# An attention block on one core: the row shift goes to GpSimd, half of the normalising to ScalarE, small jobs one step later, and image 0's opening is reordered

## What is computed

```
# block 1, per image; N = 1024 pixels
pairwise = (theta_x @ phi_x) / N;   y = pairwise @ g_x
z = x + out_w @ y + out_b
# block 2, per image; c = 128
theta = t_w @ z + t_b;  phi = p_w @ z + p_b
scores = einsum('cp,cq->pq', theta, phi) / sqrt(c)
attn = softmax(scores, axis=-1)            # 1024 x 1024
out = z + conv1_w @ einsum('pq,cq->cp', attn, z) + conv1_b
```

## Time and profile before

| | us |
|---|---|
| median of three runs | 188.06 |
| the profiled execution, its own time | 187.35 |
| its span, first to last instruction | 185.6 |
| TensorE busy | 167.1 (90%) |
| VectorE busy | 140.6 (76%) |
| ScalarE busy | 100.4 (54%) |
| GpSimd busy | 34.9 (19%) |
| chain that ended last: PE, DVE, ACT | 46%, 31%, 14% |

### The profile page before, as it was taken

How to read it: one execution, slowest core, us unless ns; L and a number is a source line. 1 busy time by engine, 2 the same in 40 slices (tenths; PEclk the granted TensorE clock), 3 DMA queues, 4 the chain that set the end, 5 groups by cost and what they waited for, 6 DMA issues and landing times.

```text
span 185.6 us, 2628 instructions
## 1 busy us (share of the span) xinstructions
PE 167.1 (90%) x969; PEld 135.7 (73%) x969; DVE 140.6 (76%) x253; ACT 100.4 (54%) x183; POOL 34.9 (19%) x34
## 2 busy tenths in 40 slices
PE   7877647979999998999999998999999989997994
PEld 7656436867787877788778776877878768766794
DVE  1514847897898889677998899577998898888712
ACT  3235544367755672478665652467765736466420
POOL 1007000005300054018100081038000070020020
PEclk9999979999999999999999999999999999999999
DMA  5630000300000010000100010000100010001011
GB/s 138 174 113 4 0 0 0 113 2 4 0 2 0 0 58 2 0 0 4 57 0 0 0 60 0 0 2 0 60 2 0 0 57 4 0 0 57 0 60 57
DMA packets 2828, 4.75 MB, mean 26 GB/s; under 512 B 448, under 2 KB 1280, under 8 KB 2816
## 3 DMA queue, kind: packets, MB, share of 16 engines
q1 hardware_dynamic: 2304, 4.39, 6.8%
q10 hardware_dynamic: 512, 0.20, 0.6%
HBM read 2.49 MB, written 2.10 MB: 25 GB/s over the span
## 4 chain that ended last, share of the span: by engine, by line
PE 46%; DVE 31%; ACT 14%; issue 4%; DMA 3%; DVEq 0%; SPq 0%; ACTq 0%
PE numer L336 11%; DVE negmax L661 11%; DVE PT_lo L684 7%; ACT P L510 7%; PE turned L316 6%; DVE P L677 4%; PE ring L220 4%; PE aux L280 3%; PE ring L222 3%; PE ring L221 3%; ACT PT_hi L518 3%; DVE t_lo L641 3%; DMA X<-x_dram 3%; DVE shift L669 3%; PE aux L343 2%
## 5 line engine op out<-in xcount | busy, mean ns | idle before, releaser
L518 ACT ACTIVATE PT_hi<-turned 128x512 fp32r<-128x512 f32 x62 | 36.9, 595 | 35.5 <-PE turned L316 35.2
L684 DVE TENSOR_TENSOR PT_lo<-turned,PT_hi 128x512 fp32r<-128x512 f32 x62 | 42.5, 685 | 8.6 <-ACT PT_hi L518 8.4
L510 ACT ACTIVATE P<-ring,shift 128x1024 f32<-128x1024 f32 x32 | 35.7, 1117 | 20.8 <-DVE shift L669 19.4
L661 DVE TENSOR_REDUCE negmax<-ring 128x1 f32<-128x1024 f32 x32 | 38.9, 1217 | 5.9 <-PE ring L222 5.7
L316 PE MATMUL turned<-identity,P 128*128 128x128 f32 x256 | 38.8, 275 | 2.4 <-DVE P L677 2.2
L316 PEld LDWEIGHTS turned<-identity,P 128*128 128x128 f32 x256 | 31.0, 141 | 12.4 <-DVE P L677 5.5
L677 DVE TENSOR_SCALAR P<-P,rden 128x1024 f32<-128x1024 f32 x32 | 28.6, 894 | 1.1
L220 PE MATMUL ring<-Z_hi,t_hi 128*128 128x512 f32 x64 | 27.8, 434 | 0.7 <-DVE t_lo L721 0.7
L221 PE MATMUL ring<-Z_hi,t_lo 128*128 128x512 f32 x64 | 25.5, 398 | 0.0
L222 PE MATMUL ring<-Z_lo,t_hi 128*128 128x512 f32 x64 | 25.4, 398 | 0.0
L336 PE MATMUL numer<-PT_hi,V_hi 128*128 128x512 f32 x56 | 24.4, 435 | 0.5 <-issue 0.3
(11 more groups left out here) (117 smaller groups left out, 203.7 us busy)
## 6 DMA issues: line engine op xcount, KB each, us to landing
out_dram<-result SPq DMA_DIRECT2D x7, 256.0 KB, 2.1
X<-x_dram SPq DMA_DIRECT2D x3, 512.0 KB, 3.4
X<-x_dram SPq DMA_DIRECT2D x2, 256.0 KB, 3.9
out_dram<-result SPq DMA_DIRECT2D x1, 192.0 KB, 1.9
w<-weights_dram SPq DMA_DIRECT2D x1, 128.0 KB, 5.3
wi<-inner_dram ACTq DMA_DIRECT2D x1, 64.2 KB, 5.6
pg_w<-pg_weights_dram ACTq DMA_DIRECT2D x1, 64.0 KB, 3.2
pg_b<-pg_bias_dram ACTq DMA_DIRECT2D x1, 64.0 KB, 5.1
```

The costliest lines, as they stand in the source:

```text
L510: nc.scalar.activation(P[:, n % P_BUFFERS, :], ring[:, n % 2, :], ACT.Exp, bias=shift[:, t:t + 1], accum_out=den[:, t:t + 1]).then_inc(pro ...
L518: nc.scalar.activation(PT_hi[:, group % GROUPS, half_chunks(half), k * TILE:(k + 1) * TILE], turned[:, columns(half)].rearrange("p (j r) - ...
L661: nc.vector.tensor_reduce(negmax[:, t:t + 1], ring[:, n % 2, :], AX.X, ALU.max, negate=True).then_inc(max_ready, 1)
L684: nc.vector.tensor_tensor(PT_lo[:, group % GROUPS, half_chunks(half), rows], turned[:, columns(half)].rearrange("p (j r) -> p j r", j=CHUN ...
```

## The change

- **Row shift.** VectorE's `row_max` is only the maximum now. The shift goes to GpSimd (`row_shift`), put first into GpSimd's step n for tile n+2, in front of the longer work, which is spread over the steps: t = 0: `finish`, high part of X; 1 and 2: low part of X by halves; 4 and 5: `split_z`; 6: `finish`; in the last image `V_last` in step 2.
- **Normalising.** VectorE multiplies columns 0 to 511 only; ScalarE the others (`norm_half`), between the exponential of tile n+2 and the high part of the second turned half. Each half has its own semaphore for TensorE's `turn`.
- **Small jobs a step later.** t = 0: for image 0 alone the value parts 1 and 2; 1: pg0, pg1; 2: MT, R; 3: A, Z0; 4: Z1; 5: t0, V0; 6: V1, V2; 7: t1.
- **Opening.** X of image 0 is not split. Z comes from the float32 block-1 matrix `AT` and X, one float32 matmul for each half. R goes ahead of the weight transposes and A ahead of the products of the weights. TP and U are copied by VectorE instead of ScalarE, U is split by GpSimd instead of VectorE, and the float32 Z is put together by GpSimd from its parts, where ScalarE copied it from PSUM. Scores of tile 0 go ahead of the first value part; value parts 1 and 2 move from ahead of the loop into its step 0. VectorE takes `norm(0)` ahead of `row_max(1)`.

The diff, cut to its core (VectorE's and ScalarE's lists of jobs change as TensorE's does):

```diff
 
 
 JOBS = ("pg0", "pg1", "MT", "R", "A", "Z0", "Z1", "t0", "V0", "V1", "V2", "t1")
-FIRST_JOBS = ("MT", "R", "A", "t1")
+FIRST_JOBS = ("MT", "R", "A", "t1", "V2")
 
 
 def aux_before(b, job):
...
@@ -260,8 +263,7 @@
 
             def job_Z(b, half):
                 pe.wait_ge(aux_free, aux_before(b, f"Z{half}"))
-                if half == 0:
-                    pe.wait_ge(x_lo, b)
+                pe.wait_ge(x_lo, (b - 1) * HALVES + half + 1)
                 affine_half(aux[:, :], half).then_inc(aux_ready, 1)
 
             def queries(b, bank, cols):
...
@@ -308,8 +310,7 @@
                 mm.then_inc(scores_ready, 1)
 
             def turn(n, half):
-                if half == 0:
-                    pe.wait_ge(probs_normed, n + 1)
+                pe.wait_ge(probs_normed[half], n + 1)
                 if n >= 1:
                     pe.wait_ge(turned_lo, (n - 1) * HALVES + half + 1)
                 for j in half_range(half):
...
@@ -357,14 +357,15 @@
             mm.then_inc(aux_ready, 1)
 
 
+            pe.wait_ge(pad_ready, 2)
+            pe.wait_ge(wi_padded, 1)
+            pe.wait_ge(wi_loaded, 16)
+            job_R(0)
             pe.wait_ge(identity_ready, 2)
             pe.wait_ge(w_loaded, 16)
             nc.tensor.transpose(turned[:, 0:C], w[:, W_T:W_T + C], identity[:, :])
             nc.tensor.transpose(turned[:, C:2 * C], w[:, W_P:W_P + C], identity[:, :]).then_inc(tp_ready, 1)
-            pe.wait_ge(pad_ready, 2)
-            pe.wait_ge(wi_padded, 1)
-            pe.wait_ge(wi_loaded, 16)
-            job_R(0)
+            job_A(0)
             pe.wait_ge(tp_copied, 1)
             pe.wait_ge(bias_loaded, 16)
             theta_b, phi_b = bias[:, B_T:B_T + 1], bias[:, B_P:B_P + 1]
@@ -374,55 +375,59 @@
             nc.tensor.matmul(UT_bank[:, C + 1:C + 2], T_w, phi_b, start=True, stop=True)
             nc.tensor.matmul(UT_bank[:, C + 2:C + 3], theta_b.broadcast_to([C, C]), phi_b,
                              start=True, stop=True).then_inc(u_ready, 1)
-            job_A(0)
-            pe.wait_ge(aux_free, aux_after(0, "A"))
+            pe.wait_ge(first_a, 1)
             for half in range(HALVES):
-                pe.wait_ge(first_x_lo, half + 1)
-                affine_half(ring[:, 1, columns(half)], half).then_inc(first_z, 1)
+                nc.tensor.matmul(ring[:, 1, columns(half)], AT[:, :], X[:, 0, columns(half)],
+                                 start=True, stop=True).then_inc(first_z, 1)
 
             pe.wait_ge(u_lo, 1)
             pe.wait_ge(first_z_lo, 1)
             queries(0, first_t_bank(0), FIRST_T[0]).then_inc(first_t, 1)
+            scores(0)
             pe.wait_ge(first_z_ready, 1)
             pe.wait_ge(vw_ready, 2)
             pe.wait_ge(conv_loaded, 16)
             value_chunks(0, numer, 0).then_inc(first_v, 1)
-            scores(0)
             queries(0, first_t_bank(1), FIRST_T[1]).then_inc(first_t, 1)
             job_t(0, 1)
-            pe.wait_ge(first_z_ready, 2)
             scores(1)
-            for part in (1, 2):
-                pe.wait_ge(first_v_lo, part)
-                value_chunks(0, numer, part).then_inc(first_v, 1)
+
+            def first_value_part():
+                pe.wait_ge(first_z_ready, 2)
+                pe.wait_ge(first_v_lo, 1)
+                value_chunks(0, numer, 1).then_inc(first_v, 1)
 
             def job_one(b, t):
-                if t == 0:
+                if t == 0 and b == 1:
+                    first_value_part()
...
@@ -528,72 +533,70 @@
                 nc.scalar.activation(attended[:, group % GROUPS, :], numer[:, :], ACT.Identity,
                                      bias=bias[:, B_C:B_C + 1]).then_inc(numer_copied, 1)
 
-            for half in range(HALVES):
-                act.wait_ge(first_loaded[half], 16)
-                nc.scalar.activation(X_hi[:, columns(half)], X[:, 0, columns(half)], ACT.Copy).then_inc(first_x_hi, 1)
+            def norm_half(n):
+                t = n % TILES
+                act.wait_ge(rden_ready, n + 1)
+                nc.scalar.activation(P[:, n % P_BUFFERS, columns(1)], P[:, n % P_BUFFERS, columns(1)], ACT.Copy,
+                                     scale=rden[:, t:t + 1]).then_inc(probs_normed[1], 1)
+
             act.wait_ge(pad_ready, 2)
             copy_MT(0)
-            act.wait_ge(tp_ready, 1)
-            nc.scalar.activation(TP[:, :], turned[:, 0:2 * C], ACT.Copy).then_inc(tp_copied, 1)
             copy_R(0)
-            act.wait_ge(u_ready, 1)
-            nc.scalar.activation(U[:, :], turned[:, BANK:BANK + C + 3], ACT.Copy, scale=SCALE).then_inc(u_copied, 1)
-            high_A(0)
+            act.wait_ge(bias_loaded, 16)
+            act.wait_ge(aux_ready, aux_after(0, "A"))
+            nc.scalar.activation(AT[:, :], aux[:, 0:C], ACT.Copy).then_inc(first_a, 1)
...
+                act.wait_ge(first_rho, part + 1)
                 high_values(0, numer, part, first_v_hi)
 
-            first_z_copy(0)
             act.wait_ge(u_copied, 1)
             first_t_high(0)
-            first_z_copy(1)
+            first_t_high(1)
+            exps(0)
             first_v_high(0)
-            first_t_high(1)
             high_t(0, 1)
-            exps(0)
+            norm_half(0)
             exps(1)
...
@@ -602,6 +605,7 @@
                     job_one(b + 1, t)
                 if n + 2 < ALL:
                     exps(n + 2)
+                norm_half(n + 1)
                 high_turned(n, 1)
                 if n >= GT and n % GT == GT - 1:
                     copy_numer(n // GT - 1)
@@ -661,21 +669,13 @@
                 nc.vector.tensor_reduce(negmax[:, t:t + 1], ring[:, n % 2, :], AX.X, ALU.max,
                                         negate=True).then_inc(max_ready, 1)
 
-                if b == 0:
-                    dve.wait_ge(first_v_lo, 1 if t < 3 else 2 if t < 6 else 3)
-                else:
-                    dve.wait_ge(aux_free, aux_after(b, "V2"))
-                dve.wait_ge(max_ready, n + 1)
-                nc.vector.tensor_scalar(shift[:, t:t + 1], negmax[:, t:t + 1], rho[:, b % 2, t:t + 1],
-                                        rho[:, b % 2, t:t + 1], ALU.subtract, ALU.add).then_inc(shift_ready, 1)
-
             def norm(n):
                 t = n % TILES
                 dve.wait_ge(probs_ready, n + 1)
                 nc.vector.reciprocal(rden[:, t:t + 1], den[:, t:t + 1]).then_inc(rden_ready, 1)
                 dve.wait_ge(rden_ready, n + 1)
-                nc.vector.tensor_scalar(P[:, n % P_BUFFERS, :], P[:, n % P_BUFFERS, :], rden[:, t:t + 1], None,
-                                        ALU.mult).then_inc(probs_normed, 1)
+                nc.vector.tensor_scalar(P[:, n % P_BUFFERS, columns(0)], P[:, n % P_BUFFERS, columns(0)],
+                                        rden[:, t:t + 1], None, ALU.mult).then_inc(probs_normed[0], 1)
 
             def low_turned(n, half):
                 group, k = divmod(n, GT)
...
+                row_terms(0, numer, part).then_inc(first_rho, 1)
+
             first_z_low(0)
+            first_z_low(1)
             first_t_low(0)
-            first_z_low(1)
+            row_max(0)
+            dve.wait_ge(u_copied, 1)
+            first_row_terms(0)
+            first_t_low(1)
+            norm(0)
+            row_max(1)
             first_v_low(0)
-            first_t_low(1)
-            row_max(0)
             low_t(0, 1)
-            row_max(1)
-            norm(0)
...
@@ -786,24 +788,42 @@
             nc.gpsimd.memset(VW[:, C + 1:C + 2], 0.0).then_inc(vw_ready, 1)
             pool.wait_ge(u_copied, 1)
             nc.gpsimd.tensor_copy(VW[:, C:C + 1], U[:, C + 1:C + 2]).then_inc(vw_ready, 1)
-
-            def split_x(b):
+            nc.gpsimd.tensor_copy(UT_hi[:, :], U[:, 0:C]).then_inc(u_hi, 1)
+            pool.wait_ge(u_hi, 1)
+            nc.gpsimd.tensor_tensor(UT_lo[:, :], U[:, 0:C], UT_hi[:, :].bitcast(F32), ALU.subtract).then_inc(u_lo, 1)
+            for half in range(HALVES):
+                pool.wait_ge(first_z_lo, half + 1)
+                nc.gpsimd.tensor_tensor(Z[:, 0, columns(half)], Z_hi[:, 0, columns(half)].bitcast(F32),
+                                        Z_lo[:, 0, columns(half)].bitcast(F32), ALU.add).then_inc(first_z_ready, 1)
+
+            def row_shift(n):
+
+                b, t = divmod(n, TILES)
+                if t in (0, 3, 6):
+                    if b == 0 and t < 6:
+                        pool.wait_ge(first_rho, t // 3 + 1)
+                    else:
+                        pool.wait_ge(aux_free, aux_after(b, f"V{t // 3}"))
+                pool.wait_ge(max_ready, n + 1)
+                nc.gpsimd.tensor_scalar(shift[:, t:t + 1], negmax[:, t:t + 1], rho[:, b % 2, t:t + 1],
+                                        rho[:, b % 2, t:t + 1], ALU.subtract, ALU.add).then_inc(shift_ready, 1)
+
+            def high_x(b):
                 pool.wait_ge(x_loaded[b], 16)
-                if b == 1:
-                    pool.wait_ge(first_z, HALVES)
```

(41 more changed lines are left out.)

158 lines of the change are left out of this document (81 added, 77 removed).

## The result

The changed kernel takes 190.35 us (median of four runs, 189.88 to 190.62) against 187.92 for the kernel before on the same chip (four runs, 187.70 to 188.66). The ratio is 1.012, 95% interval 1.0083 to 1.0157: **1.2% slower**. The forecast was 185.9, faster. The profiled execution took 190.62, its span is 188.8 us, and TensorE was granted 0.991 of its full clock in the mean, as before.

The account below looks back on a forecast made before the run. Bound: a ScalarE-VectorE latency circle in steps without jobs, 4.02 us growing to 4.63. M(10) at 64.05, plus 78.8 for two images, 23.5 for five tiles and the ending, gave span 183.45, hence 185.9 us; range 183.0 to 190.5.

Parts of the forecast that it names:

- part 2: Images with small jobs: eight steps of 4.63 us plus additions make 39.4 us an image, against 40.55 and 40.76 before.
- the circle: Steps without jobs: latency loop maximum, shift, exponential, high part, low part, next maximum; norm_half's 0.61 lengthens 4.02 to 4.63 us.
- Rival (e): ScalarE does norm_half while it would wait, so steps don't lengthen and run at TensorE's pace: about 178 us; chance 0.05.
- rival (d): GpSimd's shift at 0.19 or norm_half at 0.50, so TensorE's pace holds the images: 182.5 us; chance 0.14.
- The loss in the last image: Last image's five tiles without small jobs: 23.5 us against 20.87 before, 2.6 lost.
- the shift on GpSimd, no change: End of maximum to exponential: shift taken at 0.31 us, 0.47 with hand-overs, against 0.48 before.
- rival (a): GpSimd's shift is slow: 0.07 more a step eats the 2.15 us gain, 0.45 gives 190.2 us; chance 0.22.
- TensorE comes 1.5 us ahead to steps 1 to 3: Images with jobs: TensorE's excess of 0.9, 0.5 and 0.4 us over 4.63 hides in its lead, costing 0.15.
- V_last 0.35 late: Last image: GpSimd's 2.44 us V_last holds VectorE's half of the normalising, making it 0.35 us late, once.
- Rival (b): GpSimd's long work holds VectorE's half or the shift, 0.25 us over 15 steps: 189.6 us; chance 0.10.
- the opening: Start to tile 2's maximum: new order brings it to 23.85 us instead of 29.28, 5.4 earlier.
- Rival (c): Opening gives less: half clock for TensorE around 24 to 28 us, or longer step 0: 188.1 us; chance 0.07.

Follow-up runs that it names:

- shift_undone: The changed kernel with the row shift back on VectorE, right behind the maximum, and ScalarE's half of the normalising kept: 189.27 us, ratio 1.007 to the kernel before.
- after: The changed kernel itself, as profiled, with all parts of the change against the kernel before: 190.35 us, ratio 1.012.
- norm_behind_high: The changed kernel with ScalarE's norm_half moved behind the high part of the second turned half: 181.71 us, ratio 0.966 to the kernel before.
- guard: The changed kernel with GpSimd's long operations waiting until VectorE's half of the normalising is done: 193.35 us, ratio 1.028 to the kernel before.

## Why the prediction was wrong

The forecast summed the spans to 183.45; the span was 188.8, 5.35 more. It lies in three places, which add up: M(10) 2.28 late (66.33 against 64.05), the two images 2.71 longer (81.51 against 78.8), the five last tiles 0.37 (23.87 against 23.5). The ending was right (17.09 against 17.10).

The step that failed is the overlap in part 2: in steps 1 to 3 of an image TensorE's work was to hide in its lead, at a price of 0.15, and it cost 1.1 us an image more, since the long circle delays VectorE's copies of the small jobs and TensorE waits for them. Next come the clock in the opening (1.8) and the price of the shift.

**The mechanism of the circle was right.** The circle was lengthened by `norm_half` and by nothing else of size: 0.62 against the 0.61 taken, and shift_undone, which has it alone, shows 4.56 to 4.64 against the 4.63 forecast. Taking it out or putting it one place later brings the circle back to 4.1. Rival (e), that the circle would not grow, is refuted, and so is rival (d): neither term was cheap. (Its terms, 0.9 for each of two images and 1.2, give 182.9 and not the 182.5 written.) The loss in the last image, forecast as 2.6, was 3.0.

**Step "the shift on GpSimd, no change": mis-sized.** Taken at 0.31, it measures 365 ns in the mean of 32. Groups by line of after:

```profile
L808 POOL TENSOR_SCALAR shift<-negmax,rho 128x1 f32<-128x1 f32 x32 | 11.7, 365 | 113.6 <-DVE negmax L669 110.6
...
L677 DVE TENSOR_SCALAR P<-P,rden 128x512 f32<-128x512 f32 x32 | 27.7, 864 | 1.1
...
L539 ACT ACTIVATE P<-P,rden 128x512 f32<-128x512 f32 x32 | 22.8, 713 | 0.9 <-DVE rden L675 0.9
```

From the end of the maximum to the exponential it is 0.56 (149.61 - 149.05), where 0.47 was forecast: 0.05 more in the operation and 0.04 more in the two hand-overs, 0.10 each. I chose the value near the only 128x1 row that the trace had, a copy without scalars, and put the point of decision at 0.07 a step. The 0.08 to 0.09 measured against the kernel before is just over it, so rival (a), at 0.22, came true, but as a part only. The prediction charged the price to all 31 steps; the runs show it where the circle ends a step: with the shift back on VectorE, M(26) to M(30) takes 18.32 and not 19.08, but a full image is only 0.16 shorter. In all shift_undone puts the net price at some 0.5% or 0.9 us, of 5.35, with intervals that overlap. The Trainium skill (GPSIMD Engine Reference, Performance pitfalls for Q7 kernels) gave 0.36 by the estimate in the prediction; this trace agrees with 0.365, and the nearest row did not. What the operation spends its time on, no run here shows.

**Step "TensorE comes 1.5 us ahead to steps 1 to 3": the lead was there, what was built on it failed, and it is the largest miss.** I gave these three steps 14.65 us; they took 15.75 (5.39, 5.33, 5.03). TensorE was ahead: scores of tile 11 ended at 69.81 by their row, 1.24 before the maximum, and by tile 13 this was down to 0.04 (81.73 and 81.77). But its own steps had grown. From scores 11 to scores 14 it took 17.03, where norm_behind_high takes 16.06 (5.44, 5.46, 5.16). VectorE's part of it, and TensorE's two pg jobs and the MT job behind them, in after:

```profile
71.05 1.21 DVE L669 TENSOR_REDUCE negmax<-ring 128x1 f32<-128x1024 f32 x1
72.18 0.68 DVE L684 TENSOR_TENSOR PT_lo<-turned,PT_hi 128x512 fp32r<-128x512 f32 x1
72.78 0.68 DVE L629 TENSOR_TENSOR pgT<-aux,pg_b 128x512 f32<-128x512 f32 x1
...
75.24 0.69 DVE L684 TENSOR_TENSOR PT_lo<-turned,PT_hi 128x512 fp32r<-128x512 f32 x1 [0.92 <-ACT PT_hi L523]
75.85 0.68 DVE L629 TENSOR_TENSOR pgT<-aux,pg_b 128x512 f32<-128x512 f32 x1
76.44 1.21 DVE L669 TENSOR_REDUCE negmax<-ring 128x1 f32<-128x1024 f32 x1
```

```profile
70.09 1.06 PE L229 MATMUL aux<-pg_w,X 128*128 128x128 f32 x8
...
73.51 1.16 PE L229 MATMUL aux<-pg_w,X 128*128 128x128 f32 x8 [0.53 <-DVE pgT L629]
...
76.58 1.15 PE L235 MATMUL aux<-pgT 128*64 128x64 f32 x16
```

The first job is in its bank by 71.15, but VectorE copies it at 72.78 only, behind a maximum that the longer circle had made late, and TensorE waits for the bank till 73.51. This first wait is still hidden: the maximum of tile 12 starts 0.38 after its scores end (76.06). The second one is not. VectorE copies the second job at 75.85, behind a low part that the circle sets, and TensorE's MT job follows at 76.58. In the chain that ended last this copy is followed by TensorE alone, from 76.58 to 88.05, over the maxima of tiles 13 and 14; image 2 has the same (copy, then TensorE from 117.19 to 128.65). In norm_behind_high the copy is done early and TensorE runs through:

```profile
70.29 0.68 DVE L629 TENSOR_TENSOR pgT<-aux,pg_b 128x512 f32<-128x512 f32 x1
...
71.65 1.15 PE L235 MATMUL aux<-pgT 128*64 128x64 f32 x16
```

So a small job couples TensorE back to the circle: being ahead doesn't help an engine that must wait for a copy on the late engine. A row of before could have told: the copy at 72.65 is a piece of its chain. In the prediction each small job was counted for what it costs VectorE, never for when it frees TensorE's bank.

**Step "V_last 0.35 late": too high for the changed kernel, too low for a better one.** The timeline of GpSimd and VectorE of after there:

```profile
158.98 2.42 POOL L859 TENSOR_TENSOR V_last<-V_hi,V_lo 128x1024 f32<-128x1024 f32 x1
...
159.26 2.43 DVE L677 TENSOR_SCALAR P<-P,rden 128x512 f32<-128x512 f32 x1
```

VectorE's half ends at 161.69, 0.29 after GpSimd, and the step is 4.87, 0.16 over the circle. With the circle at 4.11 the same block makes a step of 4.88, 0.77 over: with less slack it counts for more. Rival (b) is refuted for the changed kernel: from M(2) on its normalising on VectorE is in the chain that ended last only this once, and in guard freeing VectorE of the block gave 0.12 us in the last image, while the wait for it cost 1.5 in a full one. The Trainium skill (SBUF — State Buffer, section Who interferes with whom) says that the port pair which VectorE and GpSimd share is an exclusive lock, that `tensor_scalar` can be among the operations that take it, and that the later of the two blocks fully. The rows here agree: a half that lasts 0.49 alone lasts 2.43 here.

**Step "the opening": the order right, the clock missed.** M(2) was forecast at 23.85 and came at 25.62. TensorE's matmuls of tile 0's scores in after, which answer to the 19.89 and 25.81 of the earlier trace rows:

```profile
15.91 0.50 PE L223 MATMUL ring<-Z_hi,t_hi 128*128 128x512 f32 x1 [0.90 <-DVE t_lo L714]
...
16.70 0.62 PE L223 MATMUL ring<-Z_hi,t_hi 128*128 128x512 f32 x1
17.12 0.63 PE L224 MATMUL ring<-Z_hi,t_lo 128*128 128x512 f32 x1
17.55 0.63 PE L225 MATMUL ring<-Z_lo,t_hi 128*128 128x512 f32 x1
17.97 1.50 PE L282 MATMUL numer<-VW,Z 128*128 128x130 f32 x6
```

From 16.7 they are 0.42 apart and not 0.23; the granted clock is 0.50 from 17 to 20 us. The same stretch in norm_behind_high, whose opening is the same code, has 0.23 throughout and M(2) at 23.65. Over eleven profiled executions of kernels with this opening the two go together without exception: five with the full clock from 14 to 22 us have M(2) at 23.65 to 24.27, six with 0.50 somewhere in it at 25.11 to 25.96. Rival (c) had this, at 0.07 and at another place (24 to 28 us). It falls on an execution and not on a kernel: of norm_behind_high's four executions the one at a mean clock of 0.999 took 180.34, and of the three at 0.99 two took over 182.

The kernel before has such a stretch too, of which the prediction says nothing: in its trace the clock is 0.50 from 26 to 28 us, behind TensorE's gap of 3.63, and the scores of tile 2, for which M(2) waits, are 0.42 apart:

```profile
26.69 0.78 PE L220 MATMUL ring<-Z_hi,t_hi 128*128 128x512 f32 x1
27.27 0.63 PE L221 MATMUL ring<-Z_hi,t_lo 128*128 128x512 f32 x1
27.69 0.63 PE L222 MATMUL ring<-Z_lo,t_hi 128*128 128x512 f32 x1
```

So the clock explains 1.8 us between forecast and result, but not that the changed kernel is slower than the one before. Executions at full clock throughout are rare for both, and compare alike: 188.94 us for the changed kernel (1 of 16), 186.21 and 186.34 for the one before (2 of 53), a ratio of 1.014. From M(2) to M(10) image 0 was 0.5 longer than forecast.

**The balance.** The gain of the opening and of X_lo in halves was forecast as 5.2 us by M(26), against 3.1 lost behind it. The measured loss behind it is 3.4. What failed is the gain: 0.2 us by M(26), since the long circle held TensorE back in steps 1 to 3 (1.1 an image), the clock took 1.8, and some 1.0 is left for the shift's 0.09 a step and the rest of image 0, which no run takes apart.

## What to carry to other kernels

Before moving work to the less busy engine, find the latency circle and the place in that engine's list: the same 0.71 us operation cost 8.6 us in front of a link of the circle, and nothing behind it. An engine that runs ahead is held by every shared buffer which a later engine must empty; count when each small job frees its bank, not only what it costs. Test a change of several parts by taking each one back: here one part of several turned 3% gained into 1% lost.
